# Local attention with 7x7 windows inside a four-layer kernel: two accumulating transfers a tile instead of three, waits left out, and another table of places

## The reference

```python
x = x + _L2_conv_ref(_gn(x), w_q, w_k, w_v, rel_h, rel_w)

q = jnp.einsum('bchw,oc->bohw', x, w_q)
kmap = jnp.einsum('bchw,oc->bohw', x_pad, w_k)      # x padded by 3
vmap = jnp.einsum('bchw,oc->bohw', x_pad, w_v)
kwin = _unfold2d(kmap, 7)                           # 49 shifted views
vwin = _unfold2d(vmap, 7)
kwin = jnp.concatenate([kwin[:, :half] + rel_h, kwin[:, half:] + rel_w], axis=1)
attn = jax.nn.softmax(q[..., None] * kwin, axis=-1) # over the 49, channel by channel
out = jnp.sum(attn * vwin, axis=-1)
```

## Time and profile before

| | |
|---|---|
| median of three runs | 7823.7 us |
| the profiled execution, its own time | 7822.81 us |
| its span | 7821.0 us |
| PE, DVE, POOL, ACT busy in it | 93%, 72%, 60%, 47% |
| TensorE clock granted, mean | 0.977 of full |
| the 64 tiles of this layer | from 3314.6 to 7132.2 us |

### The profile page before, as it was taken

The page is one execution under the profiler, slowest core; times in us unless marked ns, Lnnn a source line. Parts: engine busy times, 40 slices in busy tenths (PEclk is TensorE's granted clock), DMA queues, the critical chain, the costliest instruction groups (busy, mean ns, idle before and its releaser), DMA issues. The chain is left out here.

```text
span 7821.0 us, 136128 instructions
## 1 busy us (share of the span) xinstructions
PE 7267.6 (93%) x52034; PEld 6191.0 (79%) x52034; DVE 5658.2 (72%) x8853; ACT 3661.9 (47%) x7040; POOL 4728.1 (60%) x2194
## 2 busy tenths in 40 slices
PE   5999998989998999599999999999999999996999
PEld 4777776879998777378888788888888887886999
DVE  5666665334443455589999999999999999996664
ACT  3655565423332333155555555555555555554222
POOL 3555553023333000189999899999999898995332
PEclk9999998999999999799999999999999999998999
DMA  3111112865555975133323333333333233324452
GB/s 145 63 59 59 61 68 81 292 177 146 145 145 154 264 198 156 54 66 82 78 66 72 77 80 70 74 76 69 76 85 74 64 75 78 81 57 127 148 162 78
DMA packets 660646, 818.18 MB, mean 105 GB/s; under 512 B 468598, under 2 KB 501494, under 8 KB 630247
## 3 DMA queue, kind: packets, MB, share of 16 engines
q1 hardware_dynamic: 581318, 483.44, 22.1%
q0 software_dynamic: 61504, 298.03, 16.1%
q10 hardware_dynamic: 17376, 30.54, 1.1%
HBM read 397.01 MB, written 193.76 MB: 76 GB/s over the span
## 5 line engine op out<-in xcount | busy, mean ns | idle before, releaser
L1963 POOL TENSOR_TENSOR e_ev<-e_se,e_v 128x1536 f32<-128x1536 f32 (+1 forms) x832 | 3107.9, 3936 | 162.8 <-ACT e_se L1896 162.5
L2064 DVE SCALAR_TENSOR_TENSOR e_stage<-e_k,e_rl,e_qp 128x512 f32<-128x512 f32 x3136 | 2231.6, 746 | 251.1 <-ACT e_se L1896 196.5
L1896 ACT ACTIVATE e_se<-e_stage 128x512 f32<-128x512 f32 x2880 | 1708.4, 597 | 1488.7 <-PE e_stage L1707 1416.5
L1714 PE MATMUL e_pv_sum<-e_ident,e_ev 128*128 128x128 f32 x12544 | 1790.5, 273 | 4.6 <-POOL e_ev L1963 4.4
L1707 PE MATMUL e_stage<-e_top,e_minus 128*128 128x512 f32 x3136 | 1585.5, 506 | 118.1 <-DVE e_stage L2064 108.8
L1714 PEld LDWEIGHTS e_pv_sum<-e_ident,e_ev 128*128 128x128 f32 x12544 | 1479.4, 141 | 153.8 <-issue 92.6
L1714 PE MATMUL e_pe_sum<-e_ident,e_se 128*128 128x128 f32 x8448 | 1271.3, 273 | 41.3 <-ACT e_se L1896 41.3
L1714 PEld LDWEIGHTS e_pe_sum<-e_ident,e_se 128*128 128x128 f32 x8448 | 1051.8, 140 | 226.9 <-ACT e_se L1896 54.0
L911 POOL DMA_DIRECT2D agg<-c_ot x384 | 334.7, 874 | 882.0 <-ACT c_ot L989 772.4
L403 POOL TENSOR_TENSOR a_pr<-a_pr,a_rden 128x480 f32<-128x480 f32 x512 | 494.6, 987 | 544.4 <-DVE a_rden L636 544.4
L1707 PEld LDWEIGHTS e_stage<-e_top,e_minus 128*128 128x128 f32 x3136 | 596.7, 190 | 285.0 <-DVE e_stage L2064 203.8
(11 more groups left out here) (180 smaller groups left out, 12479.1 us busy)
## 6 DMA issues: line engine op xcount, KB each, us to landing
e_acc<-e_se POOLq DMA_DIRECT2D x192, 1024.0 KB, 7.3
qkv<-b_ot SPq DMA_DIRECT2D x120, 512.0 KB, 5.9
c_xt<-qkv SPq DMA_DIRECT2D x384, 160.0 KB, 3.8
agg<-c_ot POOLq DMA_DIRECT2D x384, 160.0 KB, 2.5
f_ws<-in_L_w_sets SPq DMA_DIRECT2D x32, 1152.0 KB, 7.8
a_xb<-in_x SPq DMA_DIRECT2D x24, 768.0 KB, 5.1
a_xr<-in_x SPq DMA_DIRECT2D x32, 512.0 KB, 3.8
x<-a_xr SPq DMA_DIRECT2D x32, 512.0 KB, 2.8
```

Source lines behind the costliest of these rows:

```text
L1714: last = nc.tensor.matmul(total[:, c * PART:(c + 1) * PART], lhsT=src[:, c * PART:(c + 1) * PART], rhs=ident[:], is_transpose=True, start= ...
L1896: nc.scalar.activation(exps(t, j), stage[:, bank_of(t, j), :], ACT.Exp).then_inc(exp_done, 1)
L1963: nc.gpsimd.tensor_tensor(split(ev[(t * NG2 + g) % NEV][:, 0:size]), split(exps(t, o * K2 + i, size)), window(v[h], h, u, o, i, size), ALU ...
L2064: nc.vector.scalar_tensor_tensor(rows(stage[:, bank_of(t, j), :]), win, rl[:, h, o:o + 1], rows(qp[:]), ALU.add, ALU.mult).then_inc(multip ...
```

## The change

GATHERED loses row 3: two accumulating DMAs a tile are left, and the exponentials of taps 21 to 24 are summed by PE directly. ACT no longer waits for e_summed, and POOL leaves out its wait for v_summed where the order on PE covers it. All tables of places are new.

```diff
-        PROJ_AT = ({24: 'Q1', 5: 'K1', 2: 'K0', 11: 'K2', 28: 'Q2'}, {5: 'V1', 15: 'V2', 3: 'V0'})
+        PROJ_AT = ({13: 'K2', 6: 'K1', 26: 'Q1', 31: 'Q2', 3: 'K0'}, {10: 'V2', 6: 'V1', 0: 'V0'})
-        V_AT = [13, 14, 14, 15, 17, 18, 19, 19, 20, 21, 22, 23, 23, 24, 25, 27, 28,
+        V_AT = [13, 15, 15, 16, 17, 18, 18, 19, 20, 20, 21, 23, 23, 25, 25, 26, 28,
...
-        GATHERED = (1, 2, 3)
+        GATHERED = (1, 2)
...
-        ACC_AT = (41, 44, 47, 48)
+        ACC_AT = (42, 43, 47, 48)
-        INVERT_AT = (4, 5, 6, 8)
+        INVERT_AT = (6, 9, 10, 12)
-        DIVIDE_AT, BACK_AT, ADD_AT = 13, 19, 24
-        STATS_AT = (26, 36)
+        DIVIDE_AT, BACK_AT, ADD_AT = 13, 20, 22
+        STATS_AT = (26, 33)
-        KEYS_AT, VALUES_AT, NEAR_AT, PAIRS_AT = 1, 17, 3, 22
+        KEYS_AT, VALUES_AT, NEAR_AT, PAIRS_AT = 1, 18, 3, 19
...
-        EXT_AT = [27, 29, 32, 34, 36, 38, 40, 43, 42, 44, 45, 46, 48, 50, 54, 60, 63,
+        EXT_AT = [24, 28, 29, 30, 34, 36, 38, 41, 41, 45, 46, 46, 47, 48, 50, 55, 59,
...
+        def summed_ahead(i, j):
+
+            return V_AT[i] < j
...
-                if j == 0 and (t >= 2 or not first):
-
-                    act.wait_ge(e_summed, tiles(n, t - 2, NES, NES))
-                elif i == start and j:
+                if i == start and j:
...
-                        else:
-                            act.wait_ge(e_summed, sums_made(n, t0, j0 + size - 1))
...
-                    pool.wait_ge(v_summed, tiles(n, t0, NTAP, g0 // 2 * K2 + sum(ROW_PARTS[g0 % 2])))
+                    held = g0 // 2 * K2 + sum(ROW_PARTS[g0 % 2])
+                    if not summed_ahead(held - 1, o * K2 + i + size - 1 + (t - t0) * NTAP):
+                        pool.wait_ge(v_summed, tiles(n, t0, NTAP, held))
```

More of the change, by code:

```diff
@@ L1467, in channel_attention @@
         FRESH, WAS = HALO, R2
-        PROJ_AT = ({24: 'Q1', 5: 'K1', 2: 'K0', 11: 'K2', 28: 'Q2'}, {5: 'V1', 15: 'V2', 3: 'V0'})
+        PROJ_AT = ({13: 'K2', 6: 'K1', 26: 'Q1', 31: 'Q2', 3: 'K0'}, {10: 'V2', 6: 'V1', 0: 'V0'})
         ROWS_OF = {"0": (PAD, PAD), "1": (FRESH, RT), "2": (FRESH + RT, RT)}
         E_LAG = 2
-        V_AT = [13, 14, 14, 15, 17, 18, 19, 19, 20, 21, 22, 23, 23, 24, 25, 27, 28,
-                29, 31, 32, 32, 35, 36, 36, 37, 38, 38, 39, 42, 43, 44, 44, 45, 47,
-                48, 49, 50, 50, 51, 51, 53, 53, 54, 55, 58, 58, 59, 60, 60]
-        GATHERED = (1, 2, 3)
+        V_AT = [13, 15, 15, 16, 17, 18, 18, 19, 20, 20, 21, 23, 23, 25, 25, 26, 28,
+                29, 30, 31, 32, 33, 34, 35, 35, 37, 38, 38, 40, 41, 42, 42, 43, 45,
+                45, 47, 48, 50, 52, 52, 53, 54, 55, 55, 58, 59, 59, 60, 60]
+        GATHERED = (1, 2)
         NACC = ROW_PARTS[0][1]
@@ L1486, in channel_attention @@
         NORM_AT = 30
-        KEYS_AT, VALUES_AT, NEAR_AT, PAIRS_AT = 1, 17, 3, 22
+        KEYS_AT, VALUES_AT, NEAR_AT, PAIRS_AT = 1, 18, 3, 19
         PIECES = ((0, 3), (3, 3), (6, 2))
         NEAR_FIRST = [(6, 'K0', 0, 0), (6, 'K0', 1, 0), (7, 'K0', 0, 1), (8, 'K0', 1, 1)]
[L1490 to L1493, removed]
+        NEAR = [(11, 'K1', 0, 0), (13, 'K1', 1, 0), (16, 'K1', 0, 1), (17, 'K1', 0, 2), (17, 'K1', 0, 3),
+                (19, 'K2', 0, 0), (20, 'K2', 1, 0), (21, 'K2', 0, 1), (24, 'K2', 0, 2), (25, 'K2', 0, 3),
+                (31, 'K1', 1, 1), (32, 'K1', 1, 2), (34, 'K1', 1, 3), (37, 'K2', 1, 1), (40, 'K2', 1, 2),
+                (42, 'K2', 1, 3)]
         CHAIN = (K2 + 1, K2 + 2)
@@ L1497, in channel_attention @@
         OPENS = [0, CHAIN[0], 2 * CHAIN[0], 2 * CHAIN[0] + CHAIN[1]]
-        EXT_AT = [27, 29, 32, 34, 36, 38, 40, 43, 42, 44, 45, 46, 48, 50, 54, 60, 63,
-                  65, 65, 67, 69, 72, 74, 76, 77, 80, 83, 86, 92, 93, 93, 95, 96, 96]
+        EXT_AT = [24, 28, 29, 30, 34, 36, 38, 41, 41, 45, 46, 46, 47, 48, 50, 55, 59,
+                  62, 66, 67, 69, 70, 74, 75, 75, 77, 81, 81, 83, 87, 91, 96, 97, 98]
         block = ctx.enter_context(nc.Block())
@@ L1588, in exps @@
             return buf[:, i] if taps is None else buf[:, i:i + taps]
-        def sums_made(n, t, j):
-            return tiles(n, t, NES, sum(d <= j for d in DIRECT) + sum(a < j + E_LAG for a in ACC_AT))
         def gathers(n, t, o):
```

## The result

| | before | changed |
|---|---|---|
| median, six runs each on one chip | 7824.1 us | 7779.1 us |
| lowest and highest | 7819.5, 7841.3 | 7773.6, 7781.1 |
| the profiled execution, its own time | 7822.8 | 7781.1 |
| the 64 tiles of the layer, first to last tap of DVE | 3817.6 | 3778.5 |

The ratio is 0.9939, with a 95% interval of 0.9929 to 0.9949. The forecast was 7807; the measured gain of 45 us is nearly three times the 16 forecast. In the profiled executions it is 41.7 us, of which 39.1 lie in the layer that was changed and 2.6 in layers that were not.

A forecast was written before the change was run, and what follows sets the result against it. It took t = 1 and 3 as bound by PE, t = 0 by DVE, t = 2 by both in turn. Sums +30, V2 -32 and opening halves -14 give -16 from 7822.8: 7807 us, own range 7785 to 7825.

The forecast's parts named there:

- changes between the two: Tile t = 2 is bound by PE and DVE in turn: PE needs 56.6 us, DVE 58.0, the tile takes 59.65.
- Four more sums, +30: Four more sums a tile on PE cost 1.85 us a band, +30 us in all; bounds 0 and +105.
- V2 earlier, -32: V2 five taps earlier starts the next band's load sooner, so ACT's 27.6 us of waits go: -32 us; bounds -38 and 0.
- Rival (c): The band's load lands late all the same, beside the accumulating transfers: +16 us, 7839; 13 in 100.
- Opening halves, -14: In opening halves K1 one tap later and V0, V1 six apart shorten PE's waits: -14 us; bounds -20 and -5.
- Two steps moved into u = 0: Two steps of the bound add some 1.3 us of DVE work in t = 0 and 2; nothing gained in t = 1, 3.
- The third DMA, nothing: One accumulating DMA a tile less gives POOL 58 us back in all, costed at nothing since PE is busier.
- Rival (d): POOL was a bound after all, through the buffers it frees: up to 58 us less, 7750 to 7790; 6 in 100.
- Left-out waits, nothing: The left-out waits of ACT and POOL are on engines that idle, so leaving them out gains nothing.
- (a): The extra sums on PE are paid nearly in full, as u = 1 tiles have no spare place: +59 us, 7882; 14 in 100.
- (b): The extra sums on PE are half paid, +3.5 us a band: +10 us, 7833; 20 in 100.
- (e): The added transposes on PE cost their listed duration, 0.27 us each: +230 us, 8050; 2 in 100.

The follow-up runs named there:

- e11: Changed kernel with one more DVE operation of 0.6 us at tap 30 of every u = 0 tile (t = 0 and 2): 7790.1 us, ratio to before 0.9949.
- e8: Changed kernel with two steps of the bound moved back out of u = 0 tiles (places 49 to 48, 98 to 97): 7799.3 us, ratio to before 0.9968.
- e7: Changed kernel with one accumulating DMA a tile for two and another four sums a tile on PE: 7858.1 us, ratio to before 1.0038.
- e4: Changed kernel with row 3 back in GATHERED: three DMAs, four sums a tile less on PE, new tables: 7792.3 us, ratio to before 0.9964.
- e1: Changed kernel with V2 of u = 1 tiles (t = 1 and 3) put back from tap 10 to tap 15: 7826.4 us, ratio to before 1.0004.
- e2: Kernel before with V2 of u = 1 tiles alone moved from tap 15 to tap 10: 7818.6 us, ratio to before 0.9995.
- e3: Kernel before with row 3 out of GATHERED: two DMAs, four more sums a tile on PE, old tables: 7854.4 us, ratio to before 1.0045.
- e6: Changed kernel with projections K0, K1, V0 and V1 at their old taps (2, 5, 3 and 5): 7821.6 us, ratio to before 0.9994.
- e5: Changed kernel with all left-out waits of ACT and POOL put back: 7772.6 us, ratio to before 0.9934.
- e12: Changed kernel with the two halves of the normalising split over taps 30 and 36 and all left-out waits back: 7766.4 us, ratio to before 0.9911.
- e9: Kernel before with a band's coefficients issued ahead of the two halves of x, not last: 7814.0 us, ratio to before 0.9979.

## Why the prediction fell short

**What bounds.** t = 3 is PE's, with nothing left (54.88 busy of 54.88). t = 0 is DVE's at tap 30 (e11), though not at its two ends, where 1 us of DVE's work less gained nothing (e8). t = 2 "changes between the two", of which e11 showed that tap 30 is PE's. This part held.

**Four more sums, +30: measured +8. This is the step that failed.** The counts were right (9472 rows of e_se, 128 DMAs), and so was the price of a sum, 0.44, which e7 shows. Wrong was the margin over PE's bare need. It was taken as 0.3 us in t = 3; it is 0.1. t = 0 and t = 2 were given +0.5 and +0.8 "since two full engines that change places lose something at every turn"; they took +0.34 and +0.21. t = 1 was given +0.25 and took -0.17. The prediction did see where the room comes from (three sums in taps 24 to 28, the projections among the reciprocals), and the runs confirm both places: e4 for the first, where without those sums tap 26 waits for DVE, and e1 for the second, where V2 costs 0.27 among the reciprocals and 1.76 at taps 15 and 16. It then added margins for friction that no row had shown. The largest error is t = 2's, 0.6 of the 1.3 us a band. The next is t = 1's, 0.4, for which a reason can be read: the normalising stops PE at tap 33, which took 2.10 us in the quiet t = 1 before and takes 2.14 now, while in t = 3 one more sum has made it 1.11 for 0.67. So the sum that the new tables put there is free in t = 1. This goes with the tables and not with the DMA: a quiet t = 1 is 1.6 us longer than its t = 3 with the old tables (before, e2, and e3 with two DMAs) and 1.3 with the new ones, also in the least disturbed t = 1 of e4 with three.

**V2 earlier, -32: about -36.** No single run isolates it. Read directly, the fifteen t = 1 tiles took 42.8 us more than quiet ones before, 6 of them an opening tile's share, and 2.8 now, of which 2.4; the layer's -39.1 less the band's +8 and the opening's -12 leaves -35; e2 gives -38 for all 27.6 us of waits, e3 -30 for 24.2 of them. The waits did go as said. A wait cost 1.3 times its length and not the 7.2/6.3 = 1.14 of the tile that the prediction went by: behind two short waits of 1.6 and 1.1 us, too, the granted clock was 0.69 in the next three taps, part of them at the lower level of 1.2 GHz, and these tiles lost 1.5 us on top; behind two others of 1.2 and 1.4 us it was 1.00 and nothing was lost on top. The cause was half told. The prediction credited V2 alone, and costed the DMA left out at nothing; e3 and e1 show that two DMAs with V2 late leave only 1.3 to 3.4 us of waits, and e2 that V2 early does it with three. Either is enough. Rival (c), the load late all the same, fell. The move of V2 had a second effect that is larger: its place in the new tables is worth 46 us in quiet bands (e1). Of the 4.7 us a band that the sums cost in the old tables, the new ones still pay 3.4 with V2 at tap 15 and 0.5 with V2 at tap 10.

**Opening halves, -14: -12.** PE's waits for e_pair at projections went from 13.7 us to 4.9, and those for e_v went. It is a net of several shifts: the opening t = 3, t = 0 and t = 1 tiles gained 0.7 to 1.5 us each and the layer's first tile 3.7, but the three opening t = 2 tiles take 63.5 us for 62.1. That K1's place also matters in quiet bands, 25 us (e6), was not seen.

**Two steps moved into u = 0.** Costed inside the +0.5 and +0.8, with the sentence that in t = 1 and 3 "nothing is gained". e8 shows the reverse: leaving them in the u = 1 tiles costs 0.7 to 0.9 us in each of those, and having them in u = 0 costs t = 0 and t = 2 nothing.

**The third DMA, nothing.** As POOL's time, no run contradicts it in the old tables: POOL's cover was there. As traffic it was not nothing: beside it the load was late, and without it 24.2 of the 27.6 us of waits go (e3). That term was put at nothing by looking at POOL alone, and it hit the right sum only because V2 early takes the same waits away. In the new tables PE is fast enough for the cover to end, and the DMA would cost 7 us of the layer or more (e4). Rival (d), POOL as a bound, was wrong for the kernel before and comes true in part with the new tables and three DMAs.

**Left-out waits, nothing.** Right (e5, e12).

**Rivals (a), (b) and (e).** (a) is what happened to the same edit in the old tables, where 4.7 of 7.0 us a band were paid and the kernel was 0.45% slower (e3); with the new tables it is false. (b) falls with it. (e), that transposes cost their listed duration, would have made e7's step 4.4 us a tile (16 x 0.27); it was 1.74.

**The sum.** Of the 26 us between the forecast's -16 and the -41.7 of the profiled executions, 22 are the sums, nearly 4 the load and 2.6 the other layers, less 2 to 3 at the openings. The medians are 3 us further apart than the profiled executions, which is within their scatter.

## What to carry to other kernels

In these runs, work added to the engine that bounds was nearly free at taps where it waited for another (V2, 0.27 of 1.76), and cost its full price elsewhere (e7): count both engines tap by tap, and don't add a margin for friction that no row shows. The places of two engines' work must be moved together (V2 at tap 10 for 15 was worth 46 us in the new tables and lost 39 in the old ones), so a table is tried whole, and one number of it changed alone tells little of its worth. When a rare long wait is cured, ask how many of the edits would each have cured it alone.

## What the hardware showed that was not expected

A transfer of 2 KB issued behind two large ones on SP's queue took 17.2 us to land and 1.6 us ahead of them (e9). In three of fifteen loads of the kernel before it landed some 20 us after the load's issue, within 0.3 us of an accumulating DMA that POOL had issued 11 to 12 us after the load, while the second half of x was there at 15.2 to 15.6. Without that DMA (e3) it never landed later than 15.7. What ties the small transfer to it is open.

The landing of a load is not a constant: 13.8 to 15.5 us in the other twelve, and 17.5 to 19.8 in the changed kernel. The delay starts at the load's first part. In the kernel before, the first half of x lands 5.1 to 5.9 us after the issue and the coefficients are issued at 2.8 to 3.3; in the changed kernel it is 9.0 to 10.6 and 6.3 to 8.0. There the load is issued 2.1 us after row 1's accumulating DMA and meets all of its flight (it lands at 6.1 to 7.2), while in the kernel before that one was nearly over (issued at -6.5, landed at 0.4 to 2.8). Row 2's is issued at 6.4 to 7.5 and lands at 15.5 to 19 us, for 2 to 3 and 10 to 14 before. Which of the two costs how much, no run tells apart. So some 4 of the 6 us by which V2 came earlier were eaten, and only 0 to 2 us of slack are left before the normalising.
